# Two deformable convolutions and attention on one core: a new order of the prologue, and a third dense tap for group 5 of each layer

## The reference

```python
off = make_offset(conv3x3(x, tm_w, tm_b), conv3x3(x, tr_w, tr_b))
py = row + DY[k] + off[:, k, 0];  px = col + DX[k] + off[:, k, 1]
y0, x0 = floor(py), floor(px);    wy, wx = py - y0, px - x0
cols = corner(y0, x0, (1-wy)*(1-wx)) + corner(y0, x0+1, (1-wy)*wx) \
     + corner(y0+1, x0, wy*(1-wx)) + corner(y0+1, x0+1, wy*wx)   # 0 outside the image
out = einsum('nckhw,ock->nohw', cols, w)
```

## Time and profile before

| | |
|---|---|
| median of 3 runs | 787.93 us (785.04 to 788.89) |
| the profiled execution | 789.25 us, its span 787.4 us |
| PE busy | 718.4 us (91%) |
| DVE, ACT, POOL busy | 590.4, 514.4, 462.3 us |
| mean granted clock of PE | 0.95 |

### The profile page before, as it was taken

The page is one execution under the profiler, slowest core; times in us unless marked ns, Lnnn a source line. Parts: engine busy times, 40 slices in busy tenths (PEclk is TensorE's granted clock), DMA queues, the critical chain, the costliest instruction groups (busy, mean ns, idle before and its releaser), DMA issues.

```text
span 787.4 us, 12252 instructions
## 1 busy us (share of the span) xinstructions
PE 718.4 (91%) x3379; PEld 439.9 (56%) x3379; DVE 590.4 (75%) x1605; ACT 514.4 (65%) x1285; POOL 462.3 (59%) x466
## 2 busy tenths in 40 slices
PE   7689999999889899949899999989898997899997
PEld 5455656555445445535466555545554542577786
DVE  4398879898778859469867999778775968677542
ACT  1387677787777767338776877777776755665332
POOL 3677777777777777067777777777777730000000
...
GB/s 185 309 166 233 258 196 200 200 209 201 205 203 205 206 210 196 52 214 179 236 264 201 198 203 200 195 204 204 202 204 210 203 53 0 1 1 28 1 27 55
DMA packets 55743, 132.22 MB, mean 168 GB/s; under 512 B 8399, under 2 KB 25072, under 8 KB 55676
## 3 DMA queue, kind: packets, MB, share of 16 engines
...
## 4 chain that ended last, share of the span: by engine, by line
PE 68%; DVE 11%; DMA 7%; ACT 6%; issue 5%; POOL 2%; DVEq 0%; SPq 0%; POOLq 0%; ACTq 0%
PE pair L1300 22%; PE pair L1313 9%; DMA G<-table,rowi 7%; PE bank L1439 5%; PE bank L1251 4%; PE bank L1253 4%; PE pair L1305 3%; PE pair L1286 3%; DVE V L892 2%; DVE U L892 2%; DVE nmax L1032 2%; POOL G L502 2%; PE bank L1120 2%; PE pair L1159 2%; PE pair L1421 2%
## 5 line engine op out<-in xcount | busy, mean ns | idle before, releaser
L502 POOL DMA_INDIRECT G<-table,rowi x448 | 454.4, 1014 | 174.2 <-issue 90.2
L1300 PE MATMUL pair<-ST,XT 128*128 128x512 f32 x512 | 246.5, 611 | 21.9 <-ACT CTD L629 21.9
L592 ACT ACTIVATE V<-G,wgt 128x128 f32<-128x128 f32 x448 | 178.8, 399 | 57.7 <-DMA G<-table,rowi 56.8
L594 ACT ACTIVATE U<-G,wgt 128x128 f32<-128x128 f32 x448 | 174.9, 390 | 0.0
L892 DVE SCALAR_TENSOR_TENSOR V<-G,wgt,V 128x128 f32<-128x128 f32 x448 | 155.4, 347 | 10.8 <-ACT U L594 10.8
L1300 PEld LDWEIGHTS pair<-ST,XT 128*128 128x128 f32 x512 | 98.1, 194 | 116.2 <-issue 69.6
L892 DVE SCALAR_TENSOR_TENSOR U<-G,wgt,U 128x128 f32<-128x128 f32 x448 | 155.8, 348 | 0.0
L942 DVE TENSOR_TENSOR ST<-pair,stacks 128x512 f32<-128x512 f32 x170 | 112.5, 684 | 54.1 <-PE pair L1286 53.0
L1313 PE MATMUL pair<-CT,dcn_T 128*128 128x512 f32 x224 | 115.4, 598 | 0.0
L651 ACT COPY CT<-bank 128x512 f32<-128x512 f32 x112 | 65.3, 583 | 57.5 <-PE bank L1253 45.1
L1251 PE MATMUL bank<-band,V 128*128 128x128 f32 x448 | 100.9, 276 | 0.6 <-ACT CT L651 0.6
...
## 6 DMA issues: line engine op xcount, KB each, us to landing
...
G<-table,rowi POOLq DMA_INDIRECT x448, 3.7
...
```

The costliest lines, as they stand in the source:

```text
L502: pool.indirect_dma_start(G[:, i % UNITS, r, :], None, table(n).rearrange("r (e k) -> r e k", e=2), bass.IndirectOffsetOnAxis(rowi[:, at:a ...
L592: act.activation(V[:, i % V_RING, r, :], G[:, i % UNITS, r, 0:C], ACT.Copy, scale=wgt[:, tile:tile + 1, 0])
L594: act.activation(U[:, i % V_RING, r, :], G[:, i % UNITS, r, 3 * C:4 * C], ACT.Copy, scale=wgt[:, tile:tile + 1, 3]).then_inc(scaled[l], 1)
L1300: pe.matmul(dense_acc, XT[:, g // IGROUPS * TS + t, :], ST[:, all_y % ST_RING, :], start=(t == 0), stop=(t == QT - 1)).then_inc(dense_mm[l ...
```

## The change

Group 5 of each layer has three dense taps (4, 5, 6) and six gathered ones, so a layer has 55 blocks. Each group has its own places for its hats in HP and HS: even groups at tap slot 0, odd ones at 2. The rows of groups 2 to 6 are used by another list: groups 2, 3 and 4 use 3, 3, 2, 3, 3, 2 rows in six steps, group 5 uses 3, 3, 2 three times, and each begins where the one before ends, so that from step 0 to step 52 every step has rows (before, steps 0 to 53). Group 4 thus begins three steps before its first block, group 5 four. A tap whose rows are done before its group's first block gets its conv_dense one step after that block's (`CONV_DENSE_AT`). Turns and spreads of hats are listed by hand (`HAT_OPS`), and the hats of groups 5 and 7 are made one step sooner.

In the prologue, DVE now makes image 0's weights, then only copies image 1 to XT, and makes the hats of group 0, the corner sums of block 0 and the offsets of image 1; positions(1) and sample_rows(1) come right before the loop. ACT does hats_top(0) between xt_copy(1) and z_copy(1), hats_middle(0) before u_copy(1), and scale(0) before the first hats_copy; setups 1 to 3 lie between the copies of the hats. PE does the setups between the turns and spreads of hats, turn(0) ahead of the first spread rows. The tile zeros has 128 columns in place of 512; a warm-up matmul of 512 columns becomes four of 128, and the bridge between the layers has four of these instead of six.

The diff, without the hunks that only replace `g % 2` by `HAT_AT[g]` in HP and HS:

```diff
@@ -34,7 +34,9 @@
     TILES = GROUPS * GT
 
     DENSE_FROM = TAPS // 2
-    DENSE = [2] * GROUPS
+    DENSE = [2, 2, 2, 2, 2, 3, 2, 2]
+    HAT_AT = [0 if g % 2 == 0 else min(DENSE) for g in range(GROUPS)]
+    HAT_SLOTS = max(HAT_AT[g] + DENSE[g] for g in range(GROUPS))
     MOST = max(DENSE)
     GATHER = [[k for k in range(TAPS) if not DENSE_FROM <= k < DENSE_FROM + d] for d in DENSE]
     STEPS = [len(taps) for taps in GATHER]
@@ -90,7 +92,7 @@
         band = sb("band", [P, KH, 2 * REACH + P])
         ident = band[:, 1, REACH:REACH + P]
         identb = sb("identb", [P, P], bf16)
-        zeros = sb("zeros", [P, 4 * C])
+        zeros = sb("zeros", [P, C])
         ones = sb("ones", [1, P])
         grid_i = sb("grid_i", [P, 2], i32)
         gridw = sb("gridw", [P, 1])
@@ -269,6 +271,7 @@
             return XN[l][:, n * HW + t * P:n * HW + (t + 1) * P]
 
         AHEAD = 2
+        assert AHEAD == 2
         TURN_AT = {n: 2 + 2 * (n - AHEAD) for n in range(AHEAD, N)}
         SUMS_AT = {n: TURN_AT[N - 1] + 2 + 3 * (n - AHEAD) for n in range(AHEAD, N)}
         TURN_FIRST = {at: n for n, at in TURN_AT.items()}
@@ -284,21 +287,41 @@
         GRID_AT = max(LATE_SETUP) + 4
         assert POSITIONS < FIRST[3] and max(WEIGHTS) + 3 < FIRST[4]
 
-        ROWS = [[2, 3, 3, 3, 3, 2]] + [[2, 2, 2, 2, 3, 3, 2]] * (GROUPS - 2) + [[3, 3, 2, 3, 3, 2]]
+        SLOW, QUICK = [2, 2, 2, 2, 3, 3, 2], [3, 3, 2, 3, 3, 2]
+        ROWS = [[2, 3, 3, 3, 3, 2], SLOW, QUICK, QUICK, QUICK, [3, 3, 2] * DENSE[5], SLOW, QUICK]
+        BEGIN = [FIRST[g] - (g > 0) for g in range(GROUPS)]
+        BEGIN[3], BEGIN[4], BEGIN[5] = FIRST[2] + 5, FIRST[3] + 4, FIRST[4] + 3
         USED = {}
         for g in range(GROUPS):
             assert sum(ROWS[g]) == QT * DENSE[g]
             for at, count in enumerate(ROWS[g]):
                 done = sum(ROWS[g][:at])
-                USED[FIRST[g] - (g > 0) + at] = [(g, y) for y in range(done, done + count)]
+                assert BEGIN[g] + at not in USED
+                USED[BEGIN[g] + at] = [(g, y) for y in range(done, done + count)]
         TAP_DONE = {i: (g, y // QT) for i, rows in USED.items() for g, y in rows if y % QT == QT - 1}
+        assert sorted(TAP_DONE.values()) == [(g, j) for g in range(GROUPS) for j in range(DENSE[g])]
+        CONV_DENSE_AT = {max(i, FIRST[g]): (g, j) for i, (g, j) in TAP_DONE.items()}
+        assert len(CONV_DENSE_AT) == NT and all(i < FIRST[g] + STEPS[g] - 1 for i, (g, j) in CONV_DENSE_AT.items())
+
+        HAT_OPS = {g: {0: ("turn", g + 1, 0), 2: ("spread", g + 1, 0), 4: ("turn", g + 1, 1),
+                       6: ("spread", g + 1, 1)} for g in range(GROUPS - 1)}
+        HAT_OPS[0] = {2: ("turn", 1, 0), 3: ("spread", 1, 0), 4: ("turn", 1, 1), 6: ("spread", 1, 1)}
+        HAT_OPS[2] = {0: ("turn", 3, 0), 2: ("spread", 3, 0), 4: ("turn", 3, 1), 5: ("spread", 3, 1)}
+        HAT_OPS[3] = {0: ("turn", 4, 0), 1: ("spread", 4, 0), 3: ("turn", 4, 1), 4: ("spread", 4, 1),
+                      6: ("turn", 5, 0)}
+        HAT_OPS[4] = {0: ("spread", 5, 0), 2: ("turn", 5, 1), 3: ("spread", 5, 1), 5: ("turn", 5, 2),
+                      6: ("spread", 5, 2)}
+        HAT_OPS[5] = {1: ("turn", 6, 0), 2: ("spread", 6, 0), 4: ("turn", 6, 1)}
+        HAT_OPS[6] = {0: ("spread", 6, 1), 2: ("turn", 7, 0), 3: ("spread", 7, 0), 4: ("turn", 7, 1),
+                      6: ("spread", 7, 1)}
+        assert [(g, j) for at in HAT_OPS for what, g, j in HAT_OPS[at].values() if what == "spread"] == \
+            [(g, j) for g in range(1, GROUPS) for j in range(DENSE[g])]
 
         def hat_op(i):
             g, s = BLOCKS[i]
-            if g + 1 == GROUPS:
-                return None
-            return ({2: ("turn", 0), 3: ("spread", 0), 4: ("turn", 1), 6: ("spread", 1)} if g == 0 else
-                    {0: ("turn", 0), 2: ("spread", 0), 4: ("turn", 1), 6: ("spread", 1)}).get(s)
+            return HAT_OPS.get(g, {}).get(s)
+
+        SOONER = [1 if max(DENSE[g], DENSE[g - 2]) > 2 else 0 for g in range(GROUPS)]
 
         def hats_step(i):
             if i < 2:
@@ -306,7 +329,7 @@
             g, s = BLOCKS[i]
             if g + 2 >= GROUPS:
                 return None, None
-            return g + 2, {2: "first", 4: "split", 6: "last"}.get(s)
+            return g + 2, {2: "first", 4: "split", 6: "last"}.get(s + SOONER[g + 2])
 
         def casts_step(i):
             if i < 2:
@@ -314,7 +337,7 @@
             g, s = BLOCKS[i]
             if g + 2 >= GROUPS:
                 return None, None
-            return g + 2, {3: "top", 5: "middle"}.get(s)
+            return g + 2, {3: "top", 5: "middle"}.get(s + SOONER[g + 2])
 
         def added(i):
             return sum(s in ADD_STEPS[g] for g, s in BLOCKS[:i])
@@ -573,14 +596,6 @@
                 xt_copy(0)
                 z_copy(0)
                 u_copy(0)
-                for n in range(1, AHEAD):
-                    relu_input(n)
-                    xt_copy(n)
-                    z_copy(n)
-                    u_copy(n)
-                if l == 0:
-                    for i in range(1, 4):
-                        setup(i)
 
                 def scale(i, rows):
 
@@ -634,13 +649,23 @@
                         act.wait_ge(acc_stats[l], GROUPS)
                     act.copy(A[l][:, g * BANK:(g + 1) * BANK], conv_acc).then_inc(acc_cp[l], 1)
 
+                relu_input(1)
+                xt_copy(1)
                 hats_top(0)
+                z_copy(1)
                 hats_middle(0)
-                hats_copy(0, 0)
-                column_copy(0, 0)
+                u_copy(1)
                 act.wait_ge(wgt_ready, l * N + 1)
                 scale(0, range(GTILES))
+                hats_copy(0, 0)
+                if l == 0:
+                    setup(1)
+                column_copy(0, 0)
+                if l == 0:
+                    setup(2)
                 hats_copy(0, 1)
+                if l == 0:
+                    setup(3)
                 column_copy(0, 1)
                 scale(1, range(GTILES))
                 scale(2, range(GTILES))
@@ -654,8 +679,8 @@
                             act.wait_ge(wgt_ready, l * N + BLOCKS[i + 3][0] // IGROUPS + 1)
                         scale(i + 3, range(0, GTILES // 2))
                     if i and hat_op(i - 1):
-                        what, j = hat_op(i - 1)
-                        (hats_copy if what == "turn" else column_copy)(BLOCKS[i - 1][0] + 1, j)
+                        what, made, j = hat_op(i - 1)
+                        (hats_copy if what == "turn" else column_copy)(made, j)
                     if i + 3 < NB:
                         scale(i + 3, range(GTILES // 2, GTILES))
                     if i in TAP_DONE:
@@ -874,13 +899,7 @@
                 positions(0, 1)
                 sample_rows(0, 1)
                 bilinear_weights(0)
-                for n in range(1, AHEAD):
-                    xt_copy(n)
-                    offsets(n)
-                dve.wait_ge(off_ready, l * N + AHEAD)
-                positions(1, AHEAD)
-                sample_rows(1, AHEAD)
-                dve.wait_ge(wgt_ready, l * N + 1)
+                xt_copy(1)
 
                 def corner_sums(i):
 
@@ -949,12 +968,17 @@
                 hats_first(0)
                 hats_split(0)
                 hats_last(0)
+                dve.wait_ge(wgt_ready, l * N + 1)
                 corner_sums(0)
+                offsets(1)
                 for now in USED[0]:
                     product(*now)
                 corner_sums(1)
                 add_halves(1)
                 hats_first(1)
+                dve.wait_ge(off_ready, l * N + AHEAD)
+                positions(1, AHEAD)
+                sample_rows(1, AHEAD)
                 for i, (g, s) in enumerate(BLOCKS):
                     more = i + 2 < NB
                     for now in USED.get(i + 1, ()):
@@ -1117,7 +1141,8 @@
             def warm_up(count, to=bank[0]):
 
                 for _ in range(count):
-                    pe.matmul(to, zeros[:, 0:P], zeros[:], start=True, stop=True)
+                    for c in range(0, BANK, C):
+                        pe.matmul(to[:, c:c + C], zeros[:], zeros[:], start=True, stop=True)
 
             pe.wait_ge(consts_dve, 1)
             warm_up(3)
@@ -1317,25 +1339,31 @@
                     pe.wait_ge(sel_ready, 1)
                 pe.wait_ge(identb_ready, 1)
                 turn_hats(0, 0)
+                if l == 0:
+                    setup(1)
                 spread_columns(0, 0)
                 if l == 0:
-                    pe.wait_ge(setup_cp, 4)
+                    setup(2)
+                turn_hats(0, 1)
+                if l == 0:
+                    setup(3)
+                spread_columns(0, 1)
+                turn(0)
                 pe.wait_ge(xt_dve, l * N + AHEAD)
                 pe.wait_ge(xt_act, l * N + AHEAD)
                 for now in USED[0]:
                     spread_rows(*now)
-                turn_hats(0, 1)
```

(14 more changed lines are left out.)

22 lines of the change are left out of this document (11 added, 11 removed).

## The result

The changed kernel takes **782.3 us** (median of 7 runs, 780.28 to 784.02); the kernel before, run beside it, 789.5 (7 runs, 785.04 to 791.78). The ratio is 0.9904, with an interval of 0.9886 to 0.9921: 7.2 us less, where 11 less were forecast. The time lies inside the forecast's range. Of the 5.3 us between 777 and 782.3, 1.6 are the kernel before, whose median over more runs is 789.5 and not 787.9. The miss that needs a cause is the other 3.7.

The account below looks back on a forecast made before the run. PE was taken to bound each layer's first half and tail, the gather rate the middle. Layer 0 -7.1 us, layer 1 -3.9, attention unchanged: -11.0 together, so 777 us, range 768 to 786.

Parts of the forecast that it names:

- Two bounds that take turns: Block loop: PE bounds each layer's first half and tail, gathers between; PE stands 14 us in layer 0, 19 in layer 1.
- Rival (c): Block loop: PE's standing is not usable, CTD waits recur with their clock loss; slower, 801 us; chance 0.08.
- The prologue of layer 0: Before layer 0's loop: block 0's CT copy at about 39 us, block 3 sooner by 3 us, block 4's gather wait gone.
- Rival (d): Prologue brings nothing, leaving only the removed gathers: 780 us, inside the range; chance 0.62 shared with the forecast.
- The sum of layer 0: Layer 0's last CT copy: gathers give 315.2 us, PE alone 313; the later against 322.3 is -7.1 us.
- The prologue of layer 1: Start of layer 1: 2 us gained for block 0's CT copy, lost again on VectorE; taken as 0, bounds -2 and +2.
- The lengthened gathers: Gathers beside more VectorE work: one gather (1.25 us) per 4 us of it, taken 1.7 us a layer, bounds 0 and 4.
- rival (b): Block loop: VectorE disturbs gathers more, 7 to 8 us a layer; 789 us, no change; decides from 5.4 us a block; chance 0.12.
- The tail of layer 1: Layer 1, last block's first gather to its CT copy: 13.1 us before, no change forecast.
- The attention part: The part behind the last CT copy of layer 1: taken as unchanged.
- The rule on shared access to SBUF: VectorE against gathers: products would not disturb them and corner sums become fewer, so the 1.7 us a layer would fall away.
- Case (a): Gathers not lengthened further, or long ones fall differently: 773.6 us, without two long ones a layer 766; chance 0.18.

Follow-up runs that it names:

- e5: Kernel after, with VectorE waiting before each tile's corner sums until the previous tile's have ended; ratio 0.9856 to the kernel before.
- e7: Kernel after, with only three of the four gathers of each block from block 8 on; ratio 0.9804 to the kernel before.
- e10: Kernel after, with two dense taps in group 5 and VectorE waiting between the corner sums of tiles; ratio 0.9992 to the kernel before.
- e1: Kernel before with the new prologue only, two dense taps in every group, old rows and bridge of six; ratio 0.9966 to the kernel before.
- e12: Kernel after, with a single VectorE wait in each block's corner sums, between tiles 1 and 2; 778.25 us, ratio 0.9816 to the kernel before.
- e8: Kernel after, with two dense taps in group 5 too, keeping new prologue and new spreading of rows; ratio 1.0047 to the kernel before.
- e6: Kernel after, with the dense rows of group 5's third tap multiplied for 64 of 512 columns; ratio 0.9904 to the kernel before.
- e11: Kernel after, with VectorE waiting between the corner sums of tiles in layer 1 only; ratio 0.9851 to the kernel before.
- e3: Kernel after, with six instead of four warm-up matmuls between the layers and after layer 1; ratio 0.991 to the kernel before.
- e4: Kernel before, with only the small zeros tile and four warm-up matmuls in pieces of 128 columns; ratio 0.9996 to the kernel before.
- e9: Kernel before, with VectorE waiting before each tile's corner sums until the previous tile's have ended; ratio 0.9953 to the kernel before.

## Why the prediction was right, and where it was off

**Two bounds that take turns.** Right, and the basis of the rest: filling PE's standing with dense rows worked. In layer 0, from 60 to 310 us, PE was busy for 240.2 us before and for 250 after. The unit prices hold where PE is the bound: three blocks of the new list were put at 15.3 us, and from block 18 to block 27 of layer 0 the CT copies of the kernel after, e5, e7 and e10 lie 45.96 us apart, three times 15.32. Rival (c) is refuted, CTD waits fell from 21.9 to 5.6 us.

**The prologue of layer 0.** Right. Block 0's CT copy at 38.1 (forecast 39), block 3 earlier by 3.8 (3 and 0.3), and POOL's wait at block 4 gone. In the kernel after other waits, at blocks 24 and 28, came in its place (2.1 us in all, as before). They cost nothing there, as PE ends this layer. e1 alone brought 3.3 us to the end of layer 0. Rival (d) is refuted.

**The sum of layer 0.** -6.5 for -7.1, but for another reason. I had the gathers ending it (315.2) and PE at 313. Its last block's gathers started at 301.05 (forecast 302.1), which with 13.1 would give 314.2; e7 shows the end doesn't move without a quarter of the gathers. So that the sum came out was luck in part: the right size from the bound that wasn't the later one. PE's sum was 3 us too low. About 1.3 us are arithmetic: at the prices printed, 52 turns (7 of half size) make 42.2 and not 41.7 us, and 117 spread rows 25.7 and not 24.9. The prices were those of the full clock; the granted clock from 60 to 310 us was 0.99, which can account for some 2 us more. I haven't tested that.

**The prologue of layer 1.** I took 0, bounds 2 either way. Block 0's CT copy came 10.0 us sooner, layer 1's first gather 7.4: a gain of 2.6, just outside the bounds. As I argued there, gathers bound this layer: POOL waited for nothing in it, before or after, so an earlier CT copy alone moved none of its gathers.

**The lengthened gathers: the term that was mis-sized.** I took one gather (1.25 us) per 4 us of added VectorE work, from two windows with VectorE at 44 and 36 of 50 us, and 1.7 us a layer. In layer 1 it was 3.1 us in the pair of profiles and 3.3 in the mean of eight; in layer 0 it was about nothing. The loss lies in blocks 18 to 27 of layer 1, where VectorE was already at 95% (44.9 of 47.3 us). The new lists use 8 rows in 3 steps there where 16 in 7 were used, 0.38 products a block more; at 0.6 us from start to start these are 2.1 us of VectorE work in nine blocks, for which the mean rate gives 0.7. The stretch itself shows more, 4.5 us of VectorE work, and the gathers lost 4.1 (3.1 in the mean of the profiles). A rate from windows with slack could not show that. In layer 0 the same nine blocks lost 1.5. This is the mechanism of rival (b), which named 5.4 us a block as the point from which it decides: 5.71 was reached, in 9 blocks and not in 27.

That gapless runs of VectorE's sums hold gathers is shown (e5, e12). Why the new lists of rows make more of that is argued from VectorE's share of the stretch, and not tested: PE is full there, too, and a run of sums without gaps can come from either.

Of the whole 3.7 us this term makes 1.5 in the table above. The comparison of e8 with e1 puts 3.0 on the spreading (+6.4 for +3.4), but it is uncertain by as much, and its profiles show only 3.2 us of difference in span.

**The tail of layer 1.** I took it as unchanged; it grew by 1.4 us. VectorE's products there waited 2.9 us for PE's rows, so PE was late in it. With the same lists of rows, e5, e6, e11 and e12 had tails of 12.6 to 13.1 us, and e3 14.5; and e4, with the loop of the kernel before, 14.6. So it isn't a fixed cost of the change, and 13.1 was no fixed tail.

**The attention part.** Open. 148.0 us in the profile of after, 146.4 in that of before; over the fourteen profiles it ranges from 146.1 to 148.1 without following an edit (e9, the kernel before with gaps, 148.1; e8 146.1). The medians moved by 7.2 us where the spans moved by 6.3, so 0.9 us of such a difference is chance in the pair of profiles anyway.

**The rule on shared access to SBUF.** The prediction weighed the Trainium skill, page "SBUF — State Buffer", section "Who interferes with whom": a VectorE instruction with two SBUF inputs contends with a GpSimd instruction that reads SBUF, one with at most one such input, outside the 2-port modes, doesn't. The trace agrees as to which instructions hold a gather: corner sums and hat operations with two SBUF inputs do, while batch statistics behind them let it go (0.81 against 1.42 us above). It doesn't agree with a lock for one instruction at a time: a held gather stays held over the whole run. Case (a), the better time by that rule, didn't come: the excess was as large as before (31.0 and 31.2 us) with eight gathers fewer.
